# Score matmuls of three attentions: from three bf16 parts in column tiles to two float32r parts in row tiles of 64

## Time and profile before

| | |
|---|---|
| median of 3 runs | 2816.89 us (2811.06 to 2822.78) |
| span of the profiled execution | 2813.9 us |
| busy, share of the span: PE / DVE / ACT / POOL | 93% / 82% / 61% / 28% |
| granted TensorE clock, mean over the span | 0.978 |
| DMA: hardware queue, share of 16 engines | 20.4% |

### The profile page before, as it was taken

The page is one execution under the profiler, slowest core; times in us unless marked ns, Lnnn a source line. Parts: engine busy times, 40 slices in busy tenths (PEclk is TensorE's granted clock), DMA queues, the critical chain, the costliest instruction groups (busy, mean ns, idle before and its releaser), DMA issues. The chain is left out here.

```text
span 2813.9 us, 121706 instructions
## 1 busy us (share of the span) xinstructions
PE 2628.6 (93%) x51440; PEld 1437.3 (51%) x51440; DVE 2305.2 (82%) x6003; ACT 1727.4 (61%) x3522; POOL 791.1 (28%) x1369
## 2 busy tenths in 40 slices
PE   5969999999999999999999999999999999999958
PEld 2435454645546465464645546464554646546432
DVE  5758879798898979889797988979889897988825
ACT  1725756666576666757666575766657566675725
POOL 4132422223241222423223242222324122242110
PEclk7979999999999999999999999999999999999987
DMA  3041221403112041221304122140312214132120
GB/s 98 7 125 36 79 76 32 125 25 108 55 59 89 26 135 30 89 73 36 113 25 123 43 77 79 31 125 25 110 52 67 81 29 133 29 90 73 34 71 6
DMA packets 168048, 191.30 MB, mean 68 GB/s; under 512 B 24614, under 2 KB 150736, under 8 KB 167504
## 3 DMA queue, kind: packets, MB, share of 16 engines
q1 hardware_dynamic: 163408, 175.12, 20.4%
q0 software_dynamic: 4096, 8.40, 1.0%
HBM read 84.18 MB, written 16.25 MB: 36 GB/s over the span
## 5 line engine op out<-in xcount | busy, mean ns | idle before, releaser
L1208 ACT ACTIVATE probs<-bank 128x512 f32<-128x512 f32 x2688 | 1463.7, 599 | 678.2 <-PE bank L615 670.6
L966 DVE TENSOR_REDUCE mx<-bank 128x1 f32<-128x512 f32 x2048 | 1281.2, 682 | 62.4 <-PE bank L615 49.3
L971 DVE CUSTOM_DVE_ANT_0 bank<-bank,mask 128x128 f32<-128x128 f32 (+3 forms) x1024 | 478.5, 517 | 109.2 <-PE bank L615 101.7
L615 PE MATMUL bank<-kp_B,qp_B 72*32 72x512 bf16 x4096 | 439.9, 390 | 18.5 <-DVE mx L966 9.2
L615 PE MATMUL bank<-qp_B,kp_B 74*32 74x512 bf16 x4096 | 413.5, 382 | 3.1 <-ACT probs L1208 1.7
L615 PE MATMUL bank<-qp_A,kp_A 74*32 74x512 bf16 x4096 | 408.5, 380 | 6.8 <-DVE mx L966 6.2
L615 PE MATMUL bank<-kp_A,qp_A 72*32 72x512 bf16 x4096 | 394.8, 381 | 12.4 <-DVE mx L966 7.5
L615 PE MATMUL bank<-kp_M,qp_M 72*32 72x128 bf16 (+3 forms) x4096 | 318.4, 311 | 32.0 <-DMA kp_M<-parts_k 23.5
L1353 POOL TENSOR_SCALAR nms<-mx 128x16 bf16<-128x16 f32 x192 | 39.5, 206 | 1087.1 <-DVE mx L971 509.6
L615 PE MATMUL bank<-qp_M,kp_M 74*32 74x128 bf16 (+3 forms) x4096 | 297.5, 302 | 20.0 <-DVE mx L966 15.2
L736 PE MATMUL pv<-probs,vv_B 128*32 128x512 f32 x2048 | 274.8, 594 | 1.2 <-ACT probs L1208 1.0
(11 more groups left out here) (167 smaller groups left out, 3286.4 us busy)
## 6 DMA issues: line engine op xcount, KB each, us to landing
wxs<-wx SPq DMA_DIRECT2D x112, 578.0 KB, 4.1
qp_M<-parts_q SPq DMA_DIRECT2D x144, 128.0 KB
kp_M<-parts_k SPq DMA_DIRECT2D x144, 128.0 KB
qp_A<-parts_q SPq DMA_DIRECT2D x144, 128.0 KB
qp_B<-parts_q SPq DMA_DIRECT2D x144, 128.0 KB
xp<-xq SPq DMA_DIRECT2D x16, 448.0 KB, 7.3
kp_A<-parts_k SPq DMA_DIRECT2D x144, 32.0 KB
xs<-x SPq DMA_DIRECT2D x16, 256.0 KB, 3.0
```

What stands on the lines that cost most here:

```text
L615: ins = pe.matmul(dst[at:at + n], lhsT[:, at:at + n], rhs, start=start, stop=stop, tile_position=(0, at))
L966: v.tensor_reduce(mx[:, g % 2, at:at + 1], s1[BANK[a, g, u]][:], AX.X, ALU.max) \
L971: v.tensor_tensor_reduce(bank[:, 0:keys], bank[:, 0:keys], mask[:, SEQ - keys:SEQ], 1.0, LOWEST, ALU.add, ALU.max, mx[:, g % 2, at:at + 1] ...
L1208: act.activation(probs[:, slot, :], s2[BANK2[a, g, u]][:], ACT.Exp).then_inc(sig[f"{a}_exp"], 1)
```

## The change

Queries and keys are cut into two float32r parts instead of three bf16 ones: `split` has two POOL operations instead of four, four products instead of nine, and `pack` issues four DMAs per operand instead of nine. The rows of a head now fit into 64 partitions (60 for the maxima, 64 with the two rows of the maximum; unused rows are zero), and two heads lie above each other, in partitions 0 to 63 and 64 to 127. A score unit is one matmul with 128 columns of weights on a row tile of 64 instead of four matmuls on column tiles; units go in pairs, the two of a pair on the two row tiles, into two banks. `score_max` and `score_exp` get times so that pairs stand together; a pair of exponentials waits for both banks before its first matmul. M's mask is added by two matmuls of 64 columns for each part and unit. All other steps of PE keep their own places in the table. The first batch zeroes the operands (on ACT, DVE and POOL) and loads the rows of minus ones from `pack`. The dtypes of `nmT` and `minus` follow.

```diff
-PARTS = 3
+PARTS = 2
 PRODUCTS = PARTS * PARTS
-ROWS1 = PRODUCTS * HD
-SHIFT = ROWS1
-ROWS2 = SHIFT + 2
+HALF = P // 2
+PAIRS = HEADS // 2
+PITCH = HALF // HD
+SHIFT = HALF - 2
+ROWS1 = SHIFT - 2
+ROWS2 = HALF
...
-                put(s + g + u / 16, "score_max", a, g, u)
+                put(s + g + u // 2 / 8, "score_max", a, g, u)
...
-                put(s + T["lag"] + g + (u + 0.5) / n, "score_exp", a, g, u)
+                put(s + T["lag"] + g + u // 2 * 2 / n, "score_exp", a, g, u)
...
-         nms=1.16, nmT=1.5, lag=1.986,
+         nms=1.16, nmT=1.5, lag=2.0,
...
-        rest = sb("rest", [P, SEQ])
-        parts = {s: sb(f"parts_{s}", [P, PARTS, SEQ], BF16) for s in "qk"}
-        qp = {a: sb(f"qp_{a}", [P, HEADS, SEQ], BF16) for a in "MBA"}
-        kp = {a: sb(f"kp_{a}", [P, kh[a], SEQ], BF16) for a in "MBA"}
+        parts = {s: sb(f"parts_{s}", [P, PARTS, SEQ], F32R) for s in "qk"}
+        qp = {a: sb(f"qp_{a}", [P, PAIRS, SEQ], F32R) for a in "MBA"}
+        kp = {a: sb(f"kp_{a}", [P, KBLOCKS[a], SEQ], F32R) for a in "MBA"}
...
         def q_rows(a, h, rows):
-            return qp[a][0:rows, h, :]
+            return qp[a][HALF * (h % 2):HALF * (h % 2) + rows, h // 2, :]
...
                 if is_q:
-                    dst, src = qp[a][r:ROWS1:PRODUCTS], parts["q"][:, r // PARTS, :]
+                    dst, src = qp[a][r:P:PITCH], parts["q"][:, r // PARTS, :]
...
             def score_max(b, a, g, u):
-                in_columns(s1[BANK[a, g, u]][:, 0:keys], q_rows(a, h, ROWS1)[:, P * t:P * t + P],
-                           k_rows(a, h, ROWS1)[:, 0:keys]).then_inc(sig[f"{a}_s1_ps"], 1)
+                pe.matmul(s1[BANK[a, g, u]][:, 0:keys], q_rows(a, h, ROWS1)[:, P * t:P * t + P],
+                          k_rows(a, h, ROWS1)[:, 0:keys], start=True, stop=True).then_inc(sig[f"{a}_s1_ps"], 1)
...
             def score_exp(b, a, g, u):
+                pair = (u, u + 1)
+                for v in pair:
+                    for s_last, value in last_user(b, turn_bank, BANK2[a, g, v], f"{a}_exp", UNITS2[a] * g + v + 1):
+                        pe.wait_ge(s_last, value)
+                for both in zip(*(unit_parts(a, v) for v in pair)):
+                    ins = {}
+                    for v, (hh, c, col, q) in zip(pair, both):
+                        h = GROUP * g + hh
+                        ins[v] = pe.matmul(s2[BANK2[a, g, v]][:, col:col + q], k_rows(a, h, ROWS2)[:, P * c:P * c + P],
+                                           q_rows(a, h, ROWS2)[:, SEQ - q:SEQ], start=True, stop=a != "M")
                     if a == "M":
-                        ins = in_columns(scores[:, 0:P], identb[:], late_keys[:], False, True)
-                ins.then_inc(sig[f"{a}_s2_ps"], 1)
+                        for k in range(2):
+                            for v, (hh, c, col, q) in zip(pair, both):
+                                half = slice(HALF * (hh % 2), HALF * (hh % 2) + HALF)
+                                ins[v] = pe.matmul(s2[BANK2[a, g, v]][:, col + HALF * k:col + HALF * k + HALF],
+                                                   eye2[half, k, :], late_keys[half], start=False, stop=k == 1)
+                for v in pair:
+                    ins[v].then_inc(sig[f"{a}_s2_ps"], 1)
...
             def split(b, s):
                 chain(b, f"{s}_split", 1, pool.tensor_scalar(p[0:n, 0, :], f, 1.0, 0.0, ALU.mult, ALU.add))
-                chain(b, f"{s}_split", 2, pool.tensor_tensor(r, f, p[0:n, 0, :], ALU.subtract))
-                chain(b, f"{s}_split", 3, pool.tensor_scalar(p[0:n, 1, :], r, 1.0, 0.0, ALU.mult, ALU.add))
-                chain(b, f"{s}_split", 4, pool.tensor_tensor(p[0:n, 2, :], r, p[0:n, 1, :], ALU.subtract))
+                pool.tensor_tensor(p[0:n, 1, :], f, p[0:n, 0, :].bitcast(F32), ALU.subtract).then_inc(sig[f"{s}_split"], 1)
+                if b.first and s == "mk":
+                    for m in (kp["A"], qp["B"]):
+                        pool.memset(m[:].bitcast(F32), 0.0)
+                    pool.memset(kp["B"][:].bitcast(F32), 0.0).then_inc(zero_pool, 1)
```

More of the change, by code:

```diff
@@ L28 @@
 F32 = mybir.dt.float32
+F32R = mybir.dt.float32r
 BF16 = mybir.dt.bfloat16
@@ L229, in ordered, with in_slots @@
     return sorted((t % PERIOD, order, name, args, int(t // PERIOD)) for t, order, name, args in rows)
+def in_slots(rows):
+    kinds = {"score_max": 0, "score_exp": 1}
+    return sorted(rows, key=lambda row: (int(SLOTS * row[0] + 1e-6), kinds.get(row[2], 2), row))
 def spare_users(name, *args):
@@ L255, in kernel_program @@
 def kernel_program(nc, x, w_all, w_lat, v_all, r_all, consts, wx, xq, yq, wi_up, wi_down, rope, out):
-    table = ordered()
+    table = ordered(LATE["PE"])
     assert max(row[4] for row in table) == LAST
@@ L577, in pack @@
                         sp.wait_ge(sig[f"{a}_s1_ps"], total(b.prev, f"{a}_s1_ps"))
-                    if b.first and s == "mq":
-                        sp.wait_ge(minus_set, 16 * 3)
+                    if b.first:
+                        sp.wait_ge({"mq": zero_act, "mk": zero_act, "aq": zero_dve}.get(s, zero_pool), 1)
+                    if b.first and not is_q:
+                        for n in range(2):
+                            sp.dma_start(kp[a][SHIFT + n:P:HALF].bitcast(F32),
+                                         minus[:].bitcast(F32).unsqueeze(1).broadcast_to([2, KBLOCKS[a], SEQ])) \
+                                .then_inc(minus_set[a], 16)
                 if is_q:
-                    dst, src = qp[a][r:ROWS1:PRODUCTS], parts["q"][:, r // PARTS, :]
+                    dst, src = qp[a][r:P:PITCH], parts["q"][:, r // PARTS, :]
                 else:
-                    dst, src = kp[a][r:ROWS1:PRODUCTS], parts["k"][0:KCH[a], r % PARTS, :]
-                sp.dma_start(dst, src).then_inc(sig[f"{s}_packed"], 16)
+                    dst, src = kp[a][r:P:PITCH], parts["k"][0:KCH[a], r % PARTS, :]
+                sp.dma_start(dst.bitcast(F32), src.bitcast(F32)).then_inc(sig[f"{s}_packed"], 16)
             def o_proj(b, a):
@@ L1141, in _ @@
             act.activation(table_loaded[:], half_neg[:], ACT.Exp)
+            for side in (qp, kp):
+                ins = act.activation(side["M"][:].rearrange("p h n -> p (h n)"),
+                                     half_neg[:, 0:1].broadcast_to([P, PAIRS * SEQ]), ACT.Copy, scale=0.0)
+            ins.then_inc(zero_act, 1)
             act.wait_ge(ld_w, 16 * 5)
@@ L1289, in values_setup @@
                         link(pool.memset(vv[a][:, :, h, one:one + 1], 1.0))
+                link(pool.memset(eye2[:], 0.0))
+                link(pool.memset(late_keys[:], 0.0))
+                for at in (0, HALF):
+                    half = slice(at, at + HALF)
+                    for k in range(2):
+                        eye = eye2[half, k, HALF * k:HALF * k + HALF]
+                        link(pool.affine_select(out=eye, in_=eye, compare_op=ALU.not_equal, fill=1.0, base=0,
+                                                pattern=[[-1, HALF]], channel_multiplier=1))
+                    link(pool.affine_select(out=late_keys[half], in_=late_keys[half], compare_op=ALU.is_ge, fill=MASKED,
+                                            base=0, pattern=[[1, HALF]], channel_multiplier=-1))
+                    link(pool.memset(eye2[at:at + 1], 0.0))
+                    link(pool.memset(eye2[at:at + 1, 0, HALF:P], 1.0))
+                    link(pool.memset(late_keys[at:at + 1], MASKED))
                 pool.memset(seen[:], 0.0).then_inc(setup_pool, 1)
```

73 lines of the change are left out of this document (36 added, 37 removed).

## The result

The changed kernel takes 3019.97 us (median of 4 runs, 3015.51 to 3025.09) against 2815.57 us beside it: a ratio of 1.0728, 95% interval 1.0707 to 1.075. The forecast was 2690 us, faster.

What follows compares the result with a forecast made beforehand. PE was taken to bound most windows and DVE A0, A3, B0 and B1. Window savings less changes of tiling gave -7.7 us a batch, -123 over sixteen, start -5: 2690 us against 2816.89, range 2610 to 2840.

Steps and rivals of the forecast that it cites:

- Part 1: Score streams: two units become two float32r matmuls side by side on row tiles, the pair taking 0.22 us.
- a pair at 0.22 for 0.44 saves 0.22: Scores of A and B: each pair saves 0.22 us, 3.5 us a group in A2 to B3.
- part 2: M's scores, loads of 128 weight columns included: maxima save 1.0 us a group, exponentials with masks 0.3.
- Part 3: PE's array: 152 changes of tiling a period instead of 30, 0.13 us each, adding 15.9 us.
- The model of the sum: Each of the period's twelve windows becomes the longer of PE's new need and DVE's busy time; together -9.5 us.
- part 4: Start, splits and packs beside the scores: earlier packs against zeroing and mask work, net -5 us, between -10 and +6.
- there PE has time: A pair's wait for both banks costs only where DVE is the bound, where PE has slack; no size given.
- a clock below 1.00: Sign that the forecast is wrong: granted clock under 1.00 in the middle of the run; no cost priced.
- the costly changes: Rival: each change of tiling on PE costs 0.26 us, giving 2840 us; chance 0.16, between 2785 and 2840.
- The half-rate pair: Rival: a float32r score pair takes 0.43 us, so A and B save nothing; 3070 us, chance 0.13.
- the imperfect sharing: Rival: row tiles share time imperfectly, a score pair takes 0.29 us; 2775 us, chance 0.12.

Runs made afterwards that it cites:

- b_visits_r: Kernel before with 64 extra small float32r visits to a row tile of 64 per batch: 3071.99 us, ratio 1.091.
- a_bf16: Changed kernel with its two operand parts in bf16 instead of float32r, same tiles, order and changes of tiling: 2880.21 us, ratio 1.024.
- a_pairwait: Changed kernel with each pair of maxima waiting for both banks before its first matmul: 3051.57 us, ratio 1.0848.
- b_bf16: Kernel before with two bf16 parts instead of three, over 32 and 34 rows, still in column tiles: 4846.68 us, ratio 1.7255.
- a_halfboth: Changed kernel with half of A's and B's maxima and exponentials left out: 2802.07 us, ratio 0.9951.
- a_halfmax: Changed kernel with A's and B's maxima taken over 256 of 512 keys: 2893.95 us, ratio 1.0296.
- b_visits: Kernel before with 64 extra small bf16 visits to a row tile of 64 per batch: 2988.57 us, ratio 1.0601.

## Why the prediction was wrong, step by step

**Part 1 was right in its stream and wrong in what stands around it.** A whole pair of float32r streams takes 0.23 to 0.24, close to the 0.22 taken. The step that failed is "a pair at 0.22 for 0.44 saves 0.22": it charged A and B nothing for weight loads of 128 columns (I priced such loads in part 2 alone, for M) and nothing for pairs that break. The cover that I took for granted, the stream before, is gone right behind a change of tiling: there the next float32r load stands in the open, 0.10 to 0.11 us a visit. In 59 of the 73 visits a batch it falls into "within row tiles", some 7 us of its 15.3; in the others, of one set of matmuls, into the change behind. b_visits_r and a_bf16 show it from both sides: a float32r load takes 195 ns, a bf16 one 95. The Trainium skill ("TensorE: Matmul & The Clock Gate", Weight-path perf modes) has a faster weight load for 128 columns of a type other than FP32 and does not name float32r; the 195 against 95 ns here agree with float32r going without it. About half of the other 8 us stands beside broken pairs; the rest is not told apart.

That the saved streams were summed to 33.2 us a batch and 33.4 were measured is in part luck: the sum had M's loads taken off, and the measured figure has about 4 us of matmuls running alone in broken pairs in it (in a_pairwait, where pairs of maxima are whole, streams are some 37 us below the kernel before).

**Part 3 was right.** 152 changes, and 0.105 us each against the 0.13 taken. The Trainium skill ("TensorEngine Tiling (Array Packing)", Key Properties) says that a change of tiling drains TensorE, without a price; these runs give 0.10 to 0.12, also between two tilings that differ in rows alone (b_bf16). The line "at changes" grew by 19.4 us against my 15.9, since part of the late loads falls into it (3.9 of it goes in a_bf16).

**The model of the sum failed second:** "each becomes the longer of PE's new need and DVE's busy time", and in part 4 "there PE has time". PE's need without waits came out at 161.2 us a batch, half clock included, where the forecast's own terms make 139.9 (166.9 - 9.7 - 33.2 + 15.9). By the model a PE that needs 161 against DVE's 145 would hardly wait. It waited 19.3. The wait that the model left out is the one for banks: the waits name them for some 10 us a batch after the change and 3 before, so for 7 of the 9.6 us that came on top, and the runs on six banks, the one with whole pairs and the three with fewer visits agree. How it comes about is my reading: PE asks for four banks of a ring of seven in each step of time and stands still until the later one is read; a pv cluster or a dense step queued behind gives DVE nothing new to read in the meantime, so both engines idle in turn. Of the 12.8 that stay with both engines cut (a_halfboth) the waits still name banks for 6.8; the rest is not told apart.

**Not foreseen: the clock,** 4.4 us a batch. The forecast named a clock below 1.00 as a sign of error and priced none. In the period shown the dips lie in A1 and B2, and ahead of A1's dip PE had just waited 1.26 us for mx:

```profile
1508.59 0.65 PE L714 MATMUL bank<-kp_A,qp_A 60*128 60x512 f32 x1 [1.26 <-DVE mx L995]
```

What exactly brings them is left open; in a_halfmax, with waits of 15.0, they are 0.9.

**Part 2** held for the exponentials and failed for the maxima. In the trace a pair of M's exponentials takes 0.41 us in one part and 0.53 to 0.57 in two, where 0.44 and 0.66 were priced: the four mask matmuls take 0.07, not 0.22, and the loads stand at the parts instead. A pair of maxima of 128, 256, 384 and 512 keys right behind a change takes 0.16, 0.22, 0.28 and 0.34, where 0.11, 0.11, 0.16 and 0.22 were priced: "a load is no longer than 0.16" was read from a load that was not float32r. M2 and M3 took 19.19 and 9.06 us against 17.40 and 8.71. **Part 4's start** was off by 6 us: the first maxima came 0.9 us later than before, not 5 earlier.

```profile
43.83 0.69 PE L714 MATMUL bank<-kp_M,qp_M 60*128 60x128 f32 x4 [9.13 <-DMA kp_M<-parts_k]
```

POOL's first latent step came 2.5 us late (3 expected), the split of the keys gave 1.8 back, the two issues of minus ones took 1.3 and the four packs 2.2 less. So the last pack was issued at 39.41 us, where it had been at 39.51, and then landed a microsecond later than before.

Of the rivals, the costly changes had the right side and the nearest reason, a weight load of 0.11 behind the change, but that case ends at 2840 us and has none of the waits. The half-rate pair came nearest in its time, 3070 us, and that is luck: it and the imperfect sharing are refuted by the starts 0.24 apart.

## What to carry to other kernels

Price a change of tiling with all that it uncovers: the change itself, the first weight load behind it, and the pair whose partner has no bank; here the two changes of a visit are 0.21 us and the load 0.10 more. Count the visits before the saving, and try the change's parts apart: here two bf16 parts instead of three gain 0.9% without row tiles and float32r, at fewer bits, and the whole change loses 7%. And where two engines hand banks to each other, the longer of the two busy times is a lower bound, not a forecast.

## What the hardware showed that was not expected

- Matmuls over 32 and over 34 rows behave as different tilings: 0.107 us at each unit, 0.325 instead of 0.218 from start to start at full clock, and 0.226 where two units of 32 rows follow each other.
- With these short tiles the granted clock fell to 0.67 on average, in stretches of 1.2 and of 2.4 GHz, at a PE share of 98%; with 72 and 74 rows, the added ones zero, it was 0.98, for the same columns. Whether the rows or the changes between the units bring it down was not tried apart; the 158 changes a batch of b_visits left it at 0.98, b_bf16 has about 520.
- A float32r weight load of 64 x 128 takes 189 to 195 ns, a bf16 one 95 to 100.
- Two streams of 512 columns on two row tiles take 0.22 us in bf16 and 0.23 to 0.24 in float32r: the tiles run side by side.
